# Perceiver block: the latents' 64 keys and values handled in one unit for both halves of the queries, each half on its own half of the array

## The reference

```python
x = x + xattn(ctx, layernorm(x), ...)                 # first stage, no mask
...
x = x + xattn(ctx, layernorm(x), mask, ...)           # fourth block, with mask

xn, ln_lat = layer_norm(x_ctx, g1, b1), layer_norm(latents, g2, b2)
q  = ln_lat @ Wq
kv = jnp.concatenate([xn, ln_lat], axis=1) @ Wkv      # 1601 + 64 rows
...
weight = einsum('bhld,bhnd->bhln', q * scale, k * scale)
weight = softmax(where(full_mask, weight, neg))       # latent keys are never masked
out = einsum('bhln,bhnd->bhld', weight, v)            # back to (b, 64, 1024)
return out @ Wout
```

## Time and profile before

| | |
|---|---|
| runs | median 2135.3 us of 3 (2131.09 to 2136.79) |
| the profiled execution | 2130.1 us, span 2128.4 us, mean granted TensorE clock 0.977 |
| first cross-attention stage, loop | about 70 to 850 us of the span |
| second cross-attention stage, loop | about 1174 to 1960 us of the span |
| instructions | 37367 |

### The profile page before, as it was taken

How to read it: one execution, slowest core, us unless ns; L and a number is a source line. 1 busy time by engine, 2 the same in 40 slices (tenths; PEclk the granted TensorE clock), 3 DMA queues, 4 the chain that set the end, 5 groups by cost and what they waited for, 6 DMA issues and landing times. The chain is left out here.

```text
span 2128.4 us, 37367 instructions
## 1 busy us (share of the span) xinstructions
PE 1997.2 (94%) x11706; PEld 1087.2 (51%) x11706; DVE 1710.3 (80%) x4135; ACT 1275.9 (60%) x2282; POOL 597.9 (28%) x641
## 2 busy tenths in 40 slices
PE   6999999999999999889798999999999999998886
PEld 5444444444454545533657445454545454554584
DVE  7888989898989897599566787879797978785657
ACT  3466666675757576444224786867777777776211
POOL 5434344443434430088001221212121212120000
PEclk9899999999999999999998999999999999999897
DMA  4232121222222110132104111111111111110100
GB/s 146 66 102 74 57 77 57 86 65 67 65 65 65 49 49 1 32 116 96 39 1 113 41 38 37 37 37 41 32 41 36 37 37 37 37 29 1 29 1 10
DMA packets 148169, 108.91 MB, mean 51 GB/s; under 512 B 120748, under 2 KB 136088, under 8 KB 148024
## 3 DMA queue, kind: packets, MB, share of 16 engines
q1 hardware_dynamic: 148024, 107.26, 17.6%
HBM read 65.15 MB, written 14.29 MB: 37 GB/s over the span
## 5 line engine op out<-in xcount | busy, mean ns | idle before, releaser
L1153 DVE TENSOR_TENSOR x_p_lo<-x_psum,x_p_hi 128x512 f16<-128x512 f32 (+2 forms) x896 | 603.6, 682 | 112.1 <-ACT x_psum L946 104.3
L945 ACT ACTIVATE x_p_hi<-x_psum 128x512 f16<-128x512 f32 (+2 forms) x480 | 287.0, 598 | 288.0 <-PE x_psum L801 285.6
L945 ACT ACTIVATE x_p_hi<-x_psum,x_bcol 128x512 f16<-128x512 f32 (+1 forms) x416 | 288.3, 693 | 161.9 <-PE x_psum L801 152.5
L820 PE MATMUL x_psum<-x_p_hi,x_x_both 128*128 128x512 f16 (+1 forms) x832 | 316.4, 380 | 15.8 <-DVE x_p_lo L1153 14.6
L799 PE MATMUL x_psum<-x_q,x_xT_both 128*128 128x512 f16 x832 | 316.4, 380 | 4.4 <-DMA x_q<-x_shift_rows 4.3
L800 PE MATMUL x_psum<-x_q,x_xT_both 128*128 128x512 f16 x832 | 315.3, 379 | 0.0
L801 PE MATMUL x_psum<-x_q,x_xT_both 128*128 128x512 f16 x832 | 315.3, 379 | 0.0
L822 PE MATMUL x_psum<-x_p_hi,x_x_both 128*128 128x512 f16 (+1 forms) x832 | 315.3, 379 | 0.0
L821 PE MATMUL x_psum<-x_p_lo,x_x_both 128*128 128x512 f16 (+1 forms) x832 | 315.3, 379 | 0.0
L1092 DVE CUSTOM_DVE_ANT_0 x_junk<-x_psum,x_brow 128x512 bf16<-128x512 f32 (+2 forms) x512 | 279.4, 584 | 11.4 <-PE x_psum L867 9.6
L946 ACT ACTIVATE x_psum<-x_psum 128x512 f32<-128x512 f32 (+2 forms) x480 | 285.2, 594 | 0.6
(11 more groups left out here) (439 smaller groups left out, 3230.7 us busy)
## 6 DMA issues: line engine op xcount, KB each, us to landing
x_x_both<-context_rows SPq DMA_DIRECT2D x32, 832.0 KB, 5.8
context_rows<-x_x SPq DMA_DIRECT2D x16, 832.0 KB, 3.5
x_raw<-in_ctx SPq DMA_DIRECT2D x16, 768.0 KB
ssm_c_row<-ssm_bc_rows SPq DMA_DIRECT2D x16, 512.0 KB, 4.1
ssm_b_wide<-ssm_bc_rows SPq DMA_DIRECT2D x7, 512.0 KB, 3.6
x_mrow<-in_mask_BxS_bk SPq DMA_DIRECT2D x16, 200.1 KB
x_Wkv<-in_L_xattn_Wkv SPq DMA_DIRECT2D x4, 512.0 KB, 4.7
x_xT_both<-context_rows SPq DMA_TRANSPOSE x96, 3.8
```

What stands on the lines that cost most here:

```text
L820: pe.matmul(out, v_hi, p_hi[r][rows, :], start=start, stop=False)
L945: act.activation(p_hi[r][rows, :], score[r][rows, :], ACT.Exp, scale=SCORE_UNIT, **bias).then_inc(p_hi_ready, 1)
L1153: v.tensor_tensor(p_lo[r][rows, :], score[r][rows, :], p_hi[r][rows, :], ALU.subtract).then_inc(p_lo_ready, 1)
```

## The change

The two units of the latents become one, so STEPS is 27. In the scores each half of the queries takes 64 columns of the array (the 64 keys of this batch as weights) and writes its own 64 partitions of one PSUM bank. ACT and DVE then work on all 128 partitions once. In the products, each half takes 64 rows of the array and writes its own bank of aux. As the second half's probabilities lie on the other 64 partitions, the latents are needed there too: four DMAs in the preparation copy lat_hi and lat_lo across (SP, after POOL's line 439), and POOL waits for them before its first `pair`. As 27 is no multiple of RING, the unit that used a buffer last is found by `user_before`.

```diff
-STEPS = 2 * (KT + 1)
+STEPS = 2 * KT + 1
...
-        lat_hi, lat_lo = sb("lat_hi", [P, NT, D], F16), sb("lat_lo", [P, NT, D], F16)
+        lat_hi, lat_lo = sb("lat_hi", [P, 2, NT, D], F16), sb("lat_lo", [P, 2, NT, D], F16)
...
                     else:
                         load_raw(sp, 1, 1, 0)
+                    sp.wait_ge(lat16_ready, 2)
+                    for x in (lat_hi, lat_lo):
+                        for k in range(2):
+                            here, there = (slice(L * q, L * q + L) for q in (k, 1 - k))
+                            sp.dma_start(x[there, 1, :, :], x[here, 0, :, :]).then_inc(lat_crossed, 16)
...
-    latp = [sb(f"latp{s}", [P, D], F16) for s in ("hi", "lo")]
+    latp = [sb(f"latp{s}", [P, 2, D], F16) for s in ("hi", "lo")]
...
+    def user_before(u):
+
+        return u - RING if u >= RING else LAST - (LAST - u) % RING - STEPS
...
-                if not (isinstance(half, int) and half + u < RING):
-                    pe.wait_ge(p_lo_ready, half + u - RING + 1)
+                if not (isinstance(half, int) and half + user_before(u) < 0):
+                    pe.wait_ge(p_lo_ready, half + user_before(u) + 1)
+                if j == KT:
+
+                    if par == 0:
+                        pe.wait_ge(pair_ready, i + 1)
+                    rows = slice(L * par, L * par + L)
+                    halves = [(score[u % RING][L * k:L * k + L, :].rearrange("p (c k) -> p c k", k=P),
+                               slice(k * NC_ // 2, (k + 1) * NC_ // 2)) for k in range(2)]
+                    for out, chunks in halves:
+                        pe.matmul(out, latTp[0][:, rows], q_hi[1][par][:, chunks, :], start=True, stop=False)
+                    for out, chunks in halves:
+                        pe.matmul(out, latTp[0][:, rows], q_lo[1][par][:, chunks, :], start=False, stop=False)
+                    for out, chunks in halves:
+                        ins = pe.matmul(out, latTp[1][:, rows], q_hi[1][par][:, chunks, :], start=False, stop=True)
+                    ins.then_inc(s_ready, 1)
+                    return
...
                 if j == KT:
-                    rows = slice(L * at.par, L * at.par + L)
-                    out, v_hi, v_lo, start, stop = aux[:, (u % 2) * HALF:(u % 2) * HALF + HALF], latp[0][rows, :], latp[1][rows, :], True, True
...
+                    sides = [(aux[:, k * HALF:(k + 1) * HALF], slice(L * k, L * k + L)) for k in range(2)]
+                    hi, lo = ([x[rows, (at.par + k) % 2, :] for k, (_, rows) in enumerate(sides)] for x in latp)
+                    for (out, rows), v_hi in zip(sides, hi):
+                        pe.matmul(out, v_hi, p_hi[r][rows, :], start=True, stop=False)
+                    for (out, rows), v_hi in zip(sides, hi):
+                        pe.matmul(out, v_hi, p_lo[r][rows, :], start=False, stop=False)
+                    for (out, rows), v_lo in zip(sides, lo):
+                        ins = pe.matmul(out, v_lo, p_hi[r][rows, :], start=False, stop=True)
+                    ins.then_inc(pv_done, 1)
+                    return
...
-                    if u == LAST - 1:
+                    if u == LAST:
 
                         pe.wait_ge(aux_free, at.free(("lat", 0)) - 2)
...
-                    act.wait_ge(pv_done, at.half + u - RING + 1)
+                    act.wait_ge(pv_done, at.half + user_before(u) + 1)
...
+                pool.wait_ge(held["lat_crossed"], 4 * 16)
...
-                    rows = slice(L * at.par, L * at.par + L) if j == KT else slice(0, P if j < CT else TAIL)
+                    rows = slice(0, TAIL if j == CT else P)
```

More of the change, by code:

```diff
@@ L174, in cross_attention @@
         x_stored, x_hi_ready = sem("x_stored"), sem("x_hi_ready")
+        lat_crossed = sem("lat_crossed")
         norm_steps = sem("norm_steps")
@@ L436, in _ @@
                     pool.wait_ge(lat_ready, 2)
-                    pool.tensor_copy(lat_hi[:, :, :], latx[:, :, :]).then_inc(lat16_ready, 1)
+                    pool.tensor_copy(lat_hi[:, 0, :, :], latx[:, :, :]).then_inc(lat16_ready, 1)
                     pool.wait_ge(lat16_ready, 1)
-                    pool.tensor_tensor(lat_lo[:, :, :], latx[:, :, :], lat_hi[:, :, :], ALU.subtract).then_inc(lat16_ready, 1)
+                    pool.tensor_tensor(lat_lo[:, 0, :, :], latx[:, :, :], lat_hi[:, 0, :, :], ALU.subtract).then_inc(lat16_ready, 1)
                 @block.vector
@@ L785, in scores @@
             def scores(u, par, half, b, i):
-                j, chunks = u // 2, slice((u % 2) * NC_ // 2, (u % 2 + 1) * NC_ // 2)
+                j = u // 2
                 if u == 0:
@@ L798, in scores @@
+                chunks = slice((u % 2) * NC_ // 2, (u % 2 + 1) * NC_ // 2)
+                k_hi, k_lo = xT_hi[par][:, j * P:(j + 1) * P], xT_lo[par][:, j * P:(j + 1) * P]
                 out = score[u % RING].rearrange("p (c k) -> p c k", k=P)
-                pe.matmul(out, k_hi, q_hi[s][par][:, chunks, :], start=True, stop=False)
-                pe.matmul(out, k_hi, q_lo[s][par][:, chunks, :], start=False, stop=False)
-                pe.matmul(out, k_lo, q_hi[s][par][:, chunks, :], start=False, stop=True).then_inc(s_ready, 1)
+                pe.matmul(out, k_hi, q_hi[0][par][:, chunks, :], start=True, stop=False)
@@ L803, in products @@
+                pe.matmul(out, k_hi, q_lo[0][par][:, chunks, :], start=False, stop=False)
+                pe.matmul(out, k_lo, q_hi[0][par][:, chunks, :], start=False, stop=True).then_inc(s_ready, 1)
             def products(u, at):
@@ L807, in products @@
                 if j == KT:
-                    rows = slice(L * at.par, L * at.par + L)
-                    out, v_hi, v_lo, start, stop = aux[:, (u % 2) * HALF:(u % 2) * HALF + HALF], latp[0][rows, :], latp[1][rows, :], True, True
-                else:
-                    rows = slice(0, P if j < CT else TAIL)
-                    out, v_hi, v_lo = acc[u % 2], x_hi[at.par][rows, j, :], x_lo[at.par][rows, j, :]
-                    start, stop = j == 0, j == CT
+                    sides = [(aux[:, k * HALF:(k + 1) * HALF], slice(L * k, L * k + L)) for k in range(2)]
[8 more added lines that the diff above has]
+                    return
+                rows = slice(0, P if j < CT else TAIL)
+                out, v_hi, v_lo = acc[u % 2], x_hi[at.par][rows, j, :], x_lo[at.par][rows, j, :]
+                start, stop = j == 0, j == CT
                 if u == 0:
@@ L1039, in body @@
                     if masked:
-                        mask_col(at.n, at.npar, at.ni, None if at.first and at.par == 0 else at.half - 2)
+                        mask_col(at.n, at.npar, at.ni, None if at.first and at.par == 0 else at.half - (STEPS - 2 * KT))
                     if at.par == 0:
```

2 lines of the change are left out of this document (1 added, 1 removed).

## The result

The changed kernel is slower: 2145.8 us at the median of 5 runs (2142.4 to 2148.4) against 2131.3 of the kernel before (2129.6 to 2136.8), a ratio of 1.0048 (95% interval 1.0033 to 1.0062), 0.5% or some 10 us. The forecast was 2114, 1.0% faster.

The account below looks back on a forecast made before the run. PE sets the pace, DVE close behind. Gains of 9.9 us (second stage) and 11.3 (first, less 1.9 at the start) make 21: profiled 2130.1 becomes 2109, median 2114; 2105 to 2125 at 70%, range 2098 to 2138.

Parts of the forecast that it names:

- The halves' overlap: Latents' groups of six half-array matmuls: both halves run together, 0.65 us; without any overlap 1.29.
- the rivals' main question: Row halves overlap, column halves don't: 2124 or 2119, 8%; no overlap: 2138, 7%; loads never fetched ahead either: 2165, 7%.
- The 0.94: Each latents' group, in us: 0.65 overlapped, 0.10 for the second half, 0.19 for two changes of shape.
- The lag of the second half: In the latents' groups, the second half runs 0.10 us behind the first, one unhidden weight load.
- The 0.84: Latents' group time in us by the skill's lag of about 4 ns a tile; gain some 5 us larger.
- Items 3, 4 and 6: Gains a batch, second/first stage: even 0.73/1.05 us, odd 0.37/0.53, a stage's first and last batch 1.08.
- The doubled step: Odd batches' step 6, two max items: loses 1.05 us (second stage), 0.84 (first); rival, costs nothing: 2101, 8%.
- Item 5: Batch's end, first units reuse buffers of three units before, not four: nothing charged, 0.1 us to spare.
- a wait appears ahead of S2' or T0': Sign of being wrong: PE waits before the next batch's unit 2 scores or unit 0 products; no size given.
- item 4: Odd batches, 7 of 8: net gain 0.37 us (second stage), 0.53 (first); next batch's first scores to first products +0.20.
- Item 7: Four DMAs added at the preparation's end: 1.9 us lost in the first stage, nothing in the second.
- Slower: Outcome given 0.08; its case: half-array weights never fetched ahead and nothing overlaps, 2165 us, 7%.

Follow-up runs that it names:

- e7: The kernel before with its pair loops written out, so no jump back: 2133.9 us, ratio 0.9982 to the kernel before.
- e6: The changed kernel with its pair loops written out, so no jump back: 2110.9 us, ratio 0.9869 to the kernel before.
- e5: The changed kernel with DVE's last copy of a batch moved after the next batch's first p_lo: 2126.3 us, ratio 0.9940 to the kernel before.
- e1: The changed kernel with the load of x in odd batches held until the next batch's first p_lo: 2143.6 us, ratio 1.0037 to the kernel before.
- e2: The kernel before with the load of x issued ahead of the two transposed loads in odd batches: 2142.4 us, ratio 1.0025 to the kernel before.

## Why the prediction was wrong, point by point

- **The halves' overlap (the rivals' main question): right.** The 0.94 held both changes of shape; the 0.77 from start to start holds one, and with the other a group costs 0.86. The lag of the second half, which I took as 0.10, doesn't show. (The 0.84 worked out from the Trainium skill, "TensorE: Matmul & The Clock Gate", Part 3, is near it.)
- **Items 3, 4 and 6 (even, odd, edge batches): right together, with errors that cancel.** Pairs without a jump take 98.51 and 100.54 us, forecast 99.0 and 100.6. Against e7's 99.87 and 101.70 that is 1.36 and 1.16 a pair; forecast, against pairs with jumps, 1.10 and 1.58. That the two nearly add up (2.52 against 2.68) is luck. From the first scores to the last latents' product the second stage takes 12.0 us less in e6 than in e7, forecast 9.9, and the first 8.7, forecast 13.2, with a first turn that is 1.9 slower. The doubled step showed its wait of 0.94 (forecast 1.05).
- **Item 5 (the ring at the batch's end): the step that failed.** "Nothing is charged, with 0.1 to spare." I asked whether p_lo25 and p_lo26 would be there for S1' and S2'; they were. I didn't ask what is left between T25 and T0' once S0' and S1' lie ahead of T25, nor what T0' needs: DVE's copy of T25's sums, its jump, and p_lo0'. I listed "a wait appears ahead of S2' or T0'" among what would prove me wrong, without a price. The sum in item 4, "from S0' to T0' it is 4.37; after, 4.17", took the earlier trace rows at a turn where DVE's restart, 2.2 us behind its copy, already lay inside the 4.37: p_lo0' starts at 1569.35 and ends 0.24 us before T0'. I read the total and not what ran beside it, and put the jump at nothing. Without a jump the 4.17 is 4.10 (1560.84 - 1556.74 in e6).
- **Its size.** At a jump PE stands 2.4 to 4.4 us in the changed kernel, 2.2 to 2.5 with the load of x held back, and at six of the eight then works at a granted clock of 0.50 for 3 to 6 us. Over both loops it is 38 us by the ratios. The forecast's gain of 21 was real and lies underneath: 23 us between the medians of e6 and e7, with some 4 us of uncertainty, and 17.6 in their profiled executions (12.0 + 8.7 - 3.1 at the start).
- **Item 7 (the start): right in kind, too small.** The first scores came 3.3 us later (73.85 against 70.52), forecast 1.9. The four issues alone run from 37.60 to 40.08, 0.62 each, where I had taken 0.37 from another issue. And at the first turn the shift rows, late in both kernels, cost more: PE stands 3.89 in place of 2.48 and then works at the lower clock for 3 us.
- Slower was given 8%, for another mechanism (no overlap of the halves, which the runs rule out), and the range ended 8 us under the result.

What stays open: whose the instruction packets are, why DVE alone shows the gap (PE and ACT jump too), and e5's late start. Of the difference between DVE's gap without the load, 2.8 us in the changed kernel, and 2.2 in the one before, some 0.4 us is only where the branch stands: 0.3 us ahead of the copy's start before, 0.1 behind it after. The rest is open too.

## What to carry to other kernels

Before an order is changed at the end of a loop's body, find in the trace each engine's first instruction behind the jump, and the gap ahead of it: a gap that costs nothing today is covered by work with a length, and the change must leave that length. Shortening the bound engine's work is also shortening the cover of every other engine's fixed costs. Where the program fits, write the loop out, or put the jump where the engine waits anyway; and when pairs of identical work differ by 7 us while others are at the forecast, look at what the long ones have in common before blaming the change's own instructions.

## What the runs showed of the hardware

- Behind a jump back DVE issues nothing for 3 us or more, which leaves a gap of 2.1 to 3.05 us behind its last copy, with an 8 KB instruction packet of 0.3 to 0.55 us in it (kernel before, e1). With an 832 KB load just issued it is up to 2.3 us for the packet and 4.9 for the gap in the changed kernel, 1.4 and 3.05 in e2. In e6, without the jump, there is no gap and no such packet in the three microseconds behind the copy.
- PE's granted clock fell to 0.50, the 1.2 GHz level, behind stands of 2.17, 3.89 and 4.42 us, and stayed at 1.00, the 2.4 GHz level, behind others of 1.56, 2.48 and 2.69 (the changed kernel's jump at 1376). So the length of the stand alone doesn't decide. From the changed kernel, three windows around the end of the stand of 4.42 (the clock is the third figure from the end):

```profile
1586.00:1589.00 3.00, 0.00 (x0) 0.00 (x0) 0.73 (x2) 0.53 (x1) 3.00 (x5) 0.80 0.56 189
1589.00:1592.50 3.50, 3.31 (x8) 1.19 (x9) 2.89 (x4) 0.53 (x1) 0.94 (x4) 0.50 0.03 8
1592.50:1596.00 3.50, 3.50 (x13) 1.42 (x12) 0.36 (x1) 1.95 (x4) 0.00 (x0) 0.70 0.00 0
```

- Two f16 matmuls of 512 columns on different halves of the array, columns or rows, run together whichever order they are issued in (three of one half and then three of the other take 0.76 us, as in turns). (The Trainium skill, "TensorE: Matmul & The Clock Gate", Part 3, says in one place that a weight load overlaps matmuls in flight only where the row group differs, and in another allows a background weight buffer as well. For the two column halves, which share all rows, the trace disagrees with the first: the loads for the second pair start at 1578.45, 0.03 us behind the start of the first pair's matmuls, and the group takes 0.77.)
